# Second attention of a two-layer block: weighing and folding one step later, a written-out step order, and the operand stack filled by six larger transfers a batch

## The reference, cut to what matters

```
x: (16, 256, 128), H = 16 heads of hd = 8, R = 64
dist[i, j] = clip(j - i, -R, R) + R                      # 0 .. 128
q, k, v    = (xn @ W_qkv + b_qkv), split in heads;  q = q / sqrt(hd)
score      = q . k[j]  +  q . rel_emb_k[dist[i, j]]
attn       = softmax(score)
ctx        = attn @ v  +  sum_j attn[i, j] * rel_emb_v[dist[i, j]]
x          = x + ctx @ W_out + b_out + experts(xn)
```

## Time and profile before

| | |
|---|---|
| time, median of 3 runs | 1673.12 us (1671.77 to 1681.12) |
| time of the profiled execution | 1669.66 us |
| its span, first to last instruction | 1668.1 us |
| mean granted clock of PE | 0.968 of full speed |
| PE / DVE / ACT / POOL busy over the span | 91% / 54% / 44% / 18% |
| DMA queue of SP | 167.18 MB |

### The profile page before, as it was taken

One profiled execution on the slowest core, in us unless ns is written; L12 is line 12 of the kernel. 1 busy time (PEld: TensorE's weight loads), 2 busy tenths in 40 slices (PEclk: granted clock), 3 DMA queues, 4 the chain that ended last, 5 costly groups with the idle time before them and its releaser, 6 DMA issues. The chain is left out here.

```text
span 1668.1 us, 37804 instructions
## 1 busy us (share of the span) xinstructions
PE 1516.5 (91%) x13904; PEld 1220.0 (73%) x13912; DVE 907.6 (54%) x3195; ACT 728.7 (44%) x1975; POOL 299.8 (18%) x382
## 2 busy tenths in 40 slices
PE   6899999999999999999599999948898898988987
PEld 5568888888888888888356656527777776777776
DVE  5336545454545454545322222227777788777876
ACT  2322222222222222222232232338888788877885
POOL 2011201101010101010440000002422243223323
PEclk9999999999999999999799999969999999999999
DMA  4009400000000000000233232238988998888986
GB/s 119 0 7 86 104 11 6 9 6 7 3 9 2 11 1 11 0 13 1 88 114 112 78 114 76 83 107 245 245 262 240 259 253 255 240 250 233 253 248 191
DMA packets 234525, 181.45 MB, mean 109 GB/s; under 512 B 83199, under 2 KB 224409, under 8 KB 234384
## 3 DMA queue, kind: packets, MB, share of 16 engines
q1 hardware_dynamic: 229010, 167.18, 38.3%
q0 software_dynamic: 5376, 12.44, 2.5%
HBM read 103.63 MB, written 75.78 MB: 108 GB/s over the span
## 5 line engine op out<-in xcount | busy, mean ns | idle before, releaser
L1555 ACT ACTIVATE a1Pm<-a1Pm,a1nmx 128x256 f32<-128x256 f32 x512 | 255.8, 506 | 0.0
L1617 DVE CUSTOM_DVE_ANT_0 a1Pm<-a1ps_S,a1Sb 128x256 f32<-128x256 f32 x512 | 195.8, 420 | 70.8 <-issue 63.7
L771 DVE TENSOR_TENSOR a0AT<-a0ps_AM,mask 128x384 f32<-128x384 f32 x256 | 124.9, 550 | 191.8 <-PE a0ps_AM L591 191.6
L776 DVE TENSOR_TENSOR a0MT<-a0ps_AM,mask 128x384 f32<-128x384 f32 x256 | 138.3, 555 | 87.7 <-PE a0ps_AM L612 87.1
L1550 ACT ACTIVATE a1Rt<-a1ps_R 128x384 f32<-128x384 f32 x264 | 128.6, 487 | 109.7 <-PE a1ps_R L1415 95.6
L1434 PE MATMUL a1ps_T<-ident,a1Pm 128*128 128x128 f32 x1024 | 161.5, 281 | 0.3 <-ACT a1Pm L1555 0.3
L1165 DVE TENSOR_TENSOR f1hid<-f1ge,f1ps_b 128x512 f32<-128x512 f32 x80 | 55.0, 687 | 192.2 <-PE f1ps_b L1098 184.6
L1415 PE MATMUL a1ps_R<-rel_st,a1stk 72*128 72x192 bf16 x528 | 92.8, 260 | 73.4 <-ACT a1Rt L1550 36.4
L610 PE MATMUL a0ps_AM<-a0AT 128*128 128x256 f32 x512 | 152.9, 380 | 0.0
L575 PE MATMUL a0ps_qk<-xnT_all,a0w_in 128*128 (+1 forms) x512 | 138.3, 393 | 2.0 <-PEq L151 1.3
L718 ACT ACTIVATE a0qk<-a0ps_qk 128x512 f32<-128x512 f32 x128 | 76.4, 597 | 116.5 <-PE a0ps_qk L575 116.5
(11 more groups left out here) (248 smaller groups left out, 2991.8 us busy)
## 6 DMA issues: line engine op xcount, KB each, us to landing
skew<-a1Rt SPq DMA_DIRECT2D x132, 384.0 KB, 4.8
a1Sb<-skew SPq DMA_DIRECT2D x131, 384.0 KB, 5.0
a1stk<-parts SPq DMA_DIRECT2D x153, 64.0 KB
a1stk<-parts SPq DMA_DIRECT2D x51, 192.0 KB
parts<-a1prt SPq DMA_DIRECT2D x18, 384.0 KB, 5.6
f1w<-in_L_ffn_w_kernel SPq DMA_DIRECT2D x16, 344.0 KB, 2.8
f1w<-in_L_ffn_w_kernel SPq DMA_DIRECT2D x16, 320.0 KB, 3.2
f1wo<-in_L_ffn_wo_kernel SPq DMA_DIRECT2D x16, 320.0 KB, 4.3
```

Source lines behind the costliest of these rows:

```text
L771: nc.vector.tensor_tensor(AT[i][h][:, :], ps_AM[i][h][:, 0:HB], mask[:, :], ALU.mult).then_inc(A_ready, 1)
L776: nc.vector.tensor_tensor(MT[i][h][:, :], ps_AM[i][h][:, 0:HB], mask[:, :], ALU.mult).then_inc(M_ready, 1)
L1555: nc.scalar.activation(Pm[:, place(h), :], Pm[:, place(h), :], ACT.Exp, bias=nmx[it][:, h:h + 1], scale=-1.0, accum_out=den[it][:, h:h + 1 ...
L1617: nc.vector.tensor_tensor_reduce(out=Pm[:, place(h), :], in0=ps_S[hp % 2][:, n, :], in1=bias_of(it, hp, n), scale=-1.0, scalar=3.0e38, op0 ...
```

## The change

1. The layout of the projected queries and keys becomes (d, h) in place of (h, d). For it POOL makes a reordered copy `w_qk` of two thirds of `w_in` once, in the first attention stage, and the bias is loaded by eight DMAs in place of one. The rows of `rel_st` are ordered to match.
2. `send_parts` writes three DMAs (queries, the first two parts of the queries again, keys), 512 KB in place of 384 KB. Each block of 24 rows of the stack is then one contiguous piece of DRAM, so `stack_queries` is three DMAs of 24 rows in place of nine of 8, all at the head of SP's step; `stack_keys` moves from the second step of a batch to the first, behind "band 3 in".
3. `weigh` and `folds` are those of tile s - 2, at the head of the step. The values `a1vx` get a second buffer, and `keep_v` waits for an older tile.
4. The calls of a step are written out one by one on PE, ACT and DVE, in a new order.

```diff
 def send_parts(sp, front, parts, n):
     sp.wait_ge(front.sm["split"], n + 1)
-    sp.dma_start(parts, front.prt[:, :, :, :]).then_inc(front.sm["parts_out"], 16)
+    parts_q, parts_k = parts
+    for to, src in ((parts_q[0:PARTS], front.prt[:, :, 0, :]), (parts_q[PARTS:2 * PARTS - 1], front.prt[:, 0:PARTS - 1, 0, :]),
+                    (parts_k, front.prt[:, :, 1, :])):
+        sp.dma_start(to.rearrange("k p t -> p k t"), src).then_inc(front.sm["parts_out"], 16)
...
+def stack_queries(sp, front, parts, n, par):
+    sp.wait_ge(front.sm["parts_out"], (n + 1) * PSENDS)
     for c in range(PARTS):
         rows = slice(c * PARTS * HD, (c + 1) * PARTS * HD)
+        q_rows = parts[0][c:c + PARTS].rearrange("k (d h) t -> (k d) h t", d=HD)
+        sp.dma_start(front.stk[par][rows, 0, :, :], q_rows).then_inc(front.queries_in[par], 16)
...
-        vx = m.sb("a1vx", [P, 2, 2, H1, QW])
+        vx = [m.sb(f"a1vx{i}", [P, 2, 2, H1, QW]) for i in range(2)]
...
@@ PE, step @@
+                    key_scores(s, it, par, 0)
...
+                    rel_scores(s + 1, nit, npar, 0)
+                    if behind >= 2:
+                        for q in range(QUAD):
+                            weigh(s - 2, b - 1, it, q)
+                    key_scores(s, it, par, 1)
...
+                        folds(s - 2)
+                    rel_scores(s + 1, nit, npar, 3)
+                    key_scores(s, it, par, 4)
+                    transposes(s, 0)
+                    if it == 1:
+                        project_qk(b + 2)
...
@@ DVE, step @@
+                    add_scores(r, i, 6)
+                    keep_T(s, it, 3)
+                    if behind >= 1:
+                        pick_diagonal(s - 1, 1 - it, 2)
+                        pick_diagonal(s - 1, 1 - it, 3)
+                    add_scores(r, i, 7)
+                    keep_T(s, it, 5)
...
-                nc.vector.memset(vx[:, :, :, :, :], 0.0)
+                for i in range(2):
+                    nc.vector.memset(vx[i][:, :, :, :, :], 0.0)
...
@@ PE, after the last step @@
+                for q in range(QUAD):
+                    weigh(last - 1, B - 1, 0, q)
+                folds(last - 1)
...
@@ SP, step @@
-                    fill(0)
+                    if it == 0:
+                        stack_queries(sp, front, parts, r * 2 + par + 1, 1 - par)
                     send_band(s + 1, nit, 0)
                     fetch_band(s, it, 3)
                     if s >= 3:
                         store(s - 3)
-                    fill(1)
+                    if it == 0:
+                        stack_keys(sp, front, parts, r * 2 + par + 1, 1 - par)
                     send_band(s + 1, nit, 1)
                     fetch_band(s + 1, nit, 0)
-                    fill(2)
```

More of the change, by code:

```diff
@@ L1198 @@
 TAB = 2 * T - 1
-QSTACK = 16 * PARTS * PARTS
+PSENDS = 16 * 3
+QSTACK = 16 * PARTS
 KSTACK = 16 * PARTS
@@ L1312, in load_table_inputs @@
         load(edge_v[:, n, :], rel_v[row, :].partition_broadcast(P))
-    load(bq[:, :], b_qkv[0:2 * D].rearrange("(w p) -> p w", p=P))
+    for d in range(HD):
+        load(bq[d * H1:(d + 1) * H1, :], b_qkv[0:2 * D].rearrange("(w h d) -> d h w", w=2, d=HD)[d])
     load(bv[:, :], b_qkv[2 * D:3 * D].partition_broadcast(P))
@@ new lines, in step @@
+                    rel_scores(s + 1, nit, npar, 1)
+                    key_scores(s, it, par, 2)
+                    if behind >= 1:
+                        transposes(s - 1, 6)
+                        transposes(s - 1, 7)
+                    rel_scores(s + 1, nit, npar, 2)
+                    key_scores(s, it, par, 3)
+                    if behind >= 2:
+                        folds(s - 2)
+                    rel_scores(s + 1, nit, npar, 3)
+                    key_scores(s, it, par, 4)
@@ new lines, in step @@
+                    transposes(s, 0)
+                    if it == 1:
+                        project_qk(b + 2)
+                    transposes(s, 1)
+                    key_scores(s, it, par, 5)
+                    if behind >= 2:
+                        project_out(s - 2)
+                    rel_scores(s + 1, nit, npar, 4)
+                    if behind >= 1:
+                        rel_values(s - 1, prev_b, 1 - it, 0)
+                        rel_values(s - 1, prev_b, 1 - it, 1)
+                    key_scores(s, it, par, 6)
@@ new lines, in step @@
+                    rel_scores(s + 1, nit, npar, 5)
+                    transposes(s, 2)
+                    key_scores(s, it, par, 7)
+                    transposes(s, 3)
+                    rel_scores(s + 1, nit, npar, 6)
+                    if behind >= 1:
+                        rel_values(s - 1, prev_b, 1 - it, 2)
+                        rel_values(s - 1, prev_b, 1 - it, 3)
+                    transposes(s, 4)
+                    rel_scores(s + 1, nit, npar, 7)
+                    if behind >= 1:
+                        reciprocals(s - 1)
@@ L1689, in _ @@
-                nc.vector.memset(vx[:, :, :, :, :], 0.0)
+                    add_scores(r, i, 0)
+                    if it == 1:
+                        keep_v(b)
+                    add_scores(r, i, 1)
+                    if behind >= 1:
+                        invert(s - 1, 1 - it)
+                    add_scores(r, i, 2)
+                    if behind >= 1:
+                        keep_T(s - 1, 1 - it, 7)
+                    add_scores(r, i, 3)
+                    if behind >= 2:
+                        divide(s - 2)
```

159 lines of the change are left out of this document (70 added, 89 removed).

## The result

The change made the kernel a little slower: 1681.03 us median against 1672.65 us for the kernel before on the same chip, a ratio of 1.0052 with a 95% interval of 1.0035 to 1.0069. The forecast of 1636 us and its range missed it; rival 3, the late band that stops PE (34.0 us a batch, 1680 us), gives the number that came. The profiled execution took 1683.22 us, 13.6 us more than that of before.

A forecast was written before the change was run, and what follows sets the result against it. Bound taken: a batch loop through PE, ACT, POOL, SP and three DMAs. -39.6 - 1.0 + 1.8 + 3.5 = -35.3 us from 1669.66 gave 1634.4; with the median 3.5 us higher, 1636 us was predicted, range 1599 to 1667.

The forecast's parts named there:

- rival 3: Late "band 3 in" stops PE every batch and the clock falls behind it: 34.0 us a batch, 1680 us; chance 0.09.
- The projection and the split: PE's projection put at 6.0 us behind S1, and POOL's split of queries and keys done at 13.9 us.
- Sending and landing of the parts: SP's three sends right behind the split, the last at 14.9 us behind S1, landing 5.6 us later at 20.6.
- Landings behind the stack: Bands behind the stack queries on SP's queue: "band 3 in" issued at 22.5 us behind S1 and landed at 27.5.
- the other branch: Loop through "band 0 out" (4.8 us to landing), "band 0 in" (5.0 more) and 6.6 us of ACT: 31.0 us a batch.
- the first branch: Loop through "band 3 in": queries and keys ready 11.2 us behind its landing, 30.7 us a batch.
- Keys ... cost nothing there: Three key transfers ahead of "band 1 out" and "band 0 in" replace query transfers at 0.66 us: no cost, bounds 2 us either way.
- The rule of the Trainium skill: Stack transfers use 8 DMA engines before, 12 after; by this the loop would be 31.8 us and not 31.0.
- Rival 2: Longer transfers eat most of the gain, stack transfers holding bands up by 0.8: 33.0 us a batch, 1664 us; chance 0.16.
- The new order at nothing: New step order on PE, ACT and DVE counted at no gain, with 30 us kept for the range.
- Head and tail: Extra clearing on DVE at the start, +1.8 us; weighing and folding after the last step, +3.5 us; half batches, -1.0 us.
- The wait of rows 3 goes: PE's waits for the stack before a second step's first rel_scores, 24.0 us in 12 waits, disappear.

The follow-up runs named there:

- h2: Changed kernel plus twelve 128x128 products with unused results on PE ahead of the last rel_scores of each first step; 0.9965 of the kernel before.
- g1: Changed kernel with only the three key transfers moved from a batch's first step to its second, behind "band 3 in"; 0.9982 of the kernel before.
- h3: Kernel before, old step order, new six transfers in the old places: queries spread over the first step, keys at the second's head; 0.9806 of the kernel before.
- e3: Kernel before with the new layout, parts sends, six large stack transfers and SP list, but the old step order; 0.9973 of the kernel before.
- f3: Changed kernel with bands 0 out and 3 in ahead of stack queries, projection at pair 1, keys in the second step; 0.9909 of the kernel before.
- f2: Changed kernel with "band 0 out" and "band 3 in" ahead of the stack queries and projection at pair 1; 1.0189 of the kernel before.
- i2: e3 with the key transfers moved to the second step, queries still together at the first step's head; 0.9846 of the kernel before.
- h4: Changed kernel's step order with the old layout and nine and three stack transfers, projection at pair 1; 1.0031 of the kernel before.
- h1: Changed kernel with queries and keys side by side per head in the stack, giving 512-byte packets, not 8 KB; 1.0077 of the kernel before.
- g4: Changed kernel with projection at pair 1, query transfers spread over the first step, keys at the second step's head; 0.9866 of the kernel before.
- e1: Changed kernel with "band 3 in" moved to the head of SP's first step, ahead of the stack queries; 1.0141 of the kernel before.
- f1: Changed kernel with "band 0 out" and "band 3 in" both ahead of the stack queries in SP's first step; 1.0117 of the kernel before.
- f4: e3 with "band 0 out" and "band 3 in" ahead of the stack queries; 1.0159 of the kernel before.
- e2: Changed kernel with projection and keeping of queries and keys moved back to pair 1 of the second step; 0.9949 of the kernel before.
- i1: h3 with the three key transfers also spread, one at each of three places of the second step; 0.9774 of the kernel before.

## Why the prediction was wrong

- **The projection and the split** were put at 6.0 and 13.9 us behind S1. They came at 6.8 to 7.8 and 14.6 to 15.7. One us late, partly by PE's half clock.
- **Sending and landing of the parts**: right. Issued right behind the split; the first query transfer, which waits for their landing, is issued at 18.2 to 22.1 us, 20.1 on the mean, against 20.6.
- **Issue of "band 3 in"**: 22 us on the mean against 22.5, right.
- **Landings behind the stack**: the step that failed. The sum took "landed at 27.5", 5.0 us behind the issue, and for the other branch 4.8 and 5.0. Measured were 8.0 for band 3 in, which lands at 30.0, 6.6 for band 0 out, and about 7.1 for band 0 in (h2, the same list). Put into the prediction's own sum, the first branch gives 30.7 + 3.0 = 33.7 and the other 31.0 + 1.8 + 2.1 = 34.9; measured were 34.0. Step by step the first branch was issue 22.5, landing 5.0 and 3.2 us from there to the next S1; it came as 22.0, 8.0 and 4.0. That bands land late behind stack transfers that stand together is shown by g1 against the changed kernel (band 3 in 6.6 us and not 8.0) and by h3 against e3; that it costs time, by f3 against f2 and h3 and i2 against e3.
- **The price stood in the trace of before.** The medians of rows 11 go over 131 bands. Most have nothing or 64 KB pieces ahead of them, but in the second step of each batch the three keys' transfers of 192 KB stood ahead of "band 0 out" and "band 3 in" already, and these landed in 7.7 and 8.1 us on the mean of 14 batches. One of them, in SP's timeline of the kernel before:

```profile
1365.94 1.39 SPq L1281 DMA_DIRECT2D a1stk<-parts  x3
1367.38 0.41 SPq L1756 DMA_DIRECT2D skew<-a1Rt  x1
1367.84 2.00 SPq L1765 DMA_DIRECT2D a1Sb<-skew  x1
```

  and the time to landing of the last, alone in its window:

```profile
DMA to landing us min/median/max: 8.3/8.3/8.3
```

  For a band behind three transfers of 24 rows this was the nearest row, and it gives the 8 us that came after the change.
- **"Keys ... cost nothing there"**: wrong. Only the issue time on SP was counted, not the 576 KB that they put ahead of "band 1 out" and "band 0 in". The bounds of 2 us either way were too small for "band 1 out", which went from 4.2 to 8.8 us.
- **The rule of the Trainium skill** (DMA: Bandwidth & Descriptors, "Why a DMA increments its semaphore by 16 and not by 1") on engines per transfer gave 31.8 us, the right side and too little. The prediction says that nothing in the trace shows the split; the counts of packets do. SP's queue moved 408 packets of 4 bytes a batch in the changed kernel and 412 in those with the old transfers (h4). With one such packet for each engine of a transfer, 16 engines for each of the 21 or 19 other transfers leave 6 x 12 = 72 and 9 x 8 + 3 x 12 = 108, so the trace agrees with 12 and 8 engines. It does not tell whether a band waits for the bytes on all engines (576 KB at 250 GB/s, an estimated 2.4 us) or for the twelve busy ones (six packets of 0.54 us each, an estimated 3.3 us): band 0 out and band 3 in landed 2.9 and 2.8 us later than before, where 192 KB stood ahead already, and in every run with the new transfers the counts agree with twelve. h1 shows only that packets of 512 bytes in the same 24 rows do no better.
- **Rival 2** had the right mechanism (transfers hold up the bands) at 0.8 us a batch; the price was 2 to 3 us for each band.
- **Rival 3** had the right place, and its number by luck: the 3.0 us a batch on top of 31.0 were put down to the clock behind a stop. Its clock part is confirmed in kind by h2, and was 0.6 to 1 us a batch; the rest of the 34 us is bands that land late. Its chance of 0.09 was too low: the text itself said that band 3 would be some 3 us late, and put its point of decision at 2 to 3.
- **The new order at nothing**: slightly kind. e3 to the changed kernel is 0.8% (13 us) worse and h3 to g4 0.6%, and some 7 us of either would be head and tail.
- **Head and tail**: put at 1.8 + 3.5 - 1.0 = 4.3 us, came as 2.2 + 4.8 = 7.0.
- **The wait of rows 3 goes**: right.

## What to carry to other kernels

A DMA that moves from one place of a queue's list to another costs more than its issue. Here the bytes that stood together, over the rate of all engines, gave within about 1 us by how much a transfer close behind them landed later; this is an estimate that fits these runs, not a rule that they prove. Before merging or gathering transfers, list the short, awaited transfers behind them and add that time to each; if they are on the loop, put the large ones one by one into the gaps. A median time to landing holds only for the places it was measured at: look first for a transfer in the old trace that already stands behind a similar burst.

Moving the victim out of the way (e1, f1) only hands the delay to the next one in line, and can be worse. The burst itself has to be spread.

## What the runs showed of the hardware

- A band of 384 KB issued by SP's queue right behind 1.15 MB (six transfers, issued within 5 us) lands in 8.6 to 10.9 us on the mean (after, e1 to e3, f1, f2, f4, h2). Behind 0.58 MB (three transfers) the first band lands in 6.0 to 6.7 us and the next in 6.6 to 8.0 (after, e2, e3, g1, g2, h1, h2, i2), and behind the keys of before in 7.7 and 8.1. With one 192-KB transfer ahead it is some 4.5 us and 5.6 to 6.2 (g4, h3, i1), with three of 64 KB 3.7 and 5.2.
- The counts of 4-byte packets, 408 and 412 a batch, fit 12 of them for a transfer of 24 rows, 8 for one of 8 rows and 16 for one of 128.
- Filling a stop of PE with products that nobody reads raised the granted clock over 400 us from 0.92 to 0.99 and made the kernel 15 us faster, although 192 products were added. In the changed kernel it had fallen in 14 of 15 batches, at stops of PE of 1.6 to 3.6 us.
- At full clock and with no wait for DMAs, the DMA share was 0.96 in one window of 31 us at 286 GB/s; 0.9 at 250 GB/s had not been the end.
